# Which sweep takes the fourth destination block: 3, 4, 3, 3 in place of 4, 3, 3, 3 in a chain of dense graph layers

## The reference

```python
x = _layernorm(x + _L0_gnn_ref(...))   # three GCN layers, weighted edges, relu, then a linear layer
x = _layernorm(x + _L1_gnn_ref(...))   # two SAGE layers, mean over neighbours
x = _layernorm(x + _L2_gnn_ref(...))   # encoder, 5 steps of a GRU, decoder
x = _layernorm(x + _L3_gnn_ref(...))   # one GCN layer, edges counted

def step(h, w):                        # the GRU step of L2
    agg = jax.ops.segment_sum((h @ w)[src], dst, num_segments=n_nodes)
    gi, gh = agg @ gru_wih.T + gru_bih, h @ gru_whh.T + gru_bhh
    ...                                # r, z, n from the three thirds of gi and gh
    return ((1.0 - z) * n + z * h, None)
```

## Time and profile before

| | |
|---|---|
| median of three runs | 5918.23 us (5917.7 to 5918.91) |
| profiled execution | 5918.44 us, its span 5916.7 us |
| TensorE matmul busy | 4612.3 us (78%), 24881 matmuls |
| TensorE weight loads busy | 2374.8 us (40%) |
| VectorE / ScalarE / GpSimd busy | 2160.1 / 609.5 / 2625.5 us |
| build of the tables, TensorE mostly idle | until about 1458 us |
| chunk matmuls L780 | 14014 records, 3677.8 us busy |
| DMA | 1401.93 MB, mean 237 GB/s |

### The profile page before, as it was taken

The page is one execution under the profiler, slowest core; times in us unless marked ns, Lnnn a source line. Parts: engine busy times, 40 slices in busy tenths (PEclk is TensorE's granted clock), DMA queues, the critical chain, the costliest instruction groups (busy, mean ns, idle before and its releaser), DMA issues. The chain is left out here.

```text
span 5916.7 us, 76914 instructions
## 1 busy us (share of the span) xinstructions
PE 4612.3 (78%) x24881; PEld 2374.8 (40%) x24881; DVE 2160.1 (37%) x4014; ACT 609.5 (10%) x1331; POOL 2625.5 (44%) x1727
## 2 busy tenths in 40 slices
PE   1222222223999999999999999899999999998796
PEld 1222222222444444444455554444444444443343
DVE  9999999998000000011013111303022120303413
ACT  0000000000011111111111011202011020202300
POOL 3888888888788888888885000000000000000100
PEclk7555555555999999999999999999999999999897
DMA  9999953223999999999989877595867768583474
GB/s 353 357 351 352 350 109 42 36 36 82 314 292 289 297 275 300 289 297 278 300 251 273 279 260 246 162 299 174 272 215 230 249 192 298 167 279 107 132 255 140
DMA packets 717658, 1401.93 MB, mean 237 GB/s; under 512 B 268948, under 2 KB 356840, under 8 KB 692456
## 3 DMA queue, kind: packets, MB, share of 16 engines
q1 hardware_dynamic: 483832, 1346.10, 68.1%
q0 software_dynamic: 225792, 0.70, 7.7%
q10 hardware_dynamic: 7920, 53.79, 2.4%
HBM read 1160.09 MB, written 240.26 MB: 237 GB/s over the span
## 5 line engine op out<-in xcount | busy, mean ns | idle before, releaser
L780 PE MATMUL psum<-arena 128*128 128x512 f16 (+3 forms) x14014 | 3677.8, 424 | 71.1 <-DVE arena L1126 51.0
L780 PEld LDWEIGHTS psum<-arena 128*128 (+2 forms) x14014 | 1670.3, 123 | 2013.4 <-issue 938.5
L495 POOL DMA_INDIRECT W_adj<-arena x784 | 1331.8, 1699 | 295.6 <-issue 253.3
L495 POOL DMA_INDIRECT C_adj<-arena x784 | 1216.2, 1551 | 250.1 <-issue 243.0
L448 PE MATMUL psum<-arena 128*128 (+1 forms) x6664 | 224.1, 167 | 1070.6 <-DVE arena L397 1057.0
L379 DVE TENSOR_SCALAR_CACHE_REDUCE arena<-arena 128x2048 bf16<-128x2048 f32 (+15 forms) x784 | 996.9, 1342 | 0.5 <-issue 0.5
L623 POOL TENSOR_TENSOR arena<-arena 128x512 f32 (+1 forms) x13 | 22.1, 1698 | 1811.7 <-DVE arena L1115 1811.7
L448 PEld LDWEIGHTS psum<-arena 128*128 128x128 bf16 x6664 | 213.6, 104 | 1095.3 <-issue 1013.1
L1299 DVE COPY arena<-psum 128x512 f32<-128x512 f32 (+1 forms) x39 | 23.2, 654 | 1118.6 <-PE psum L790 1023.4
L1301 DVE TENSOR_SCALAR arena<-psum,arena 128x512 f32<-128x512 f32 x30 | 21.9, 748 | 1038.9 <-PE psum L780 1038.9
L621 POOL COPY arena<-arena 128x512 f32 (+1 forms) x13 | 8.0, 616 | 614.0 <-DVE arena L1115 614.0
(11 more groups left out here) (231 smaller groups left out, 2535.1 us busy)
## 6 DMA issues: line engine op xcount, KB each, us to landing
arena<-C_adj SPq DMA_DIRECT2D x784, 384.0 KB
arena<-W_adj SPq DMA_DIRECT2D x294, 768.0 KB
arena<-C_adj SPq DMA_DIRECT2D x392, 512.0 KB
arena<-W_adj SPq DMA_DIRECT2D x147, 1024.0 KB
arena<-C_adj SPq DMA_DIRECT2D x392, 288.0 KB
arena<-W_adj SPq DMA_DIRECT2D x147, 576.0 KB
W_adj<-arena SPq DMA_DIRECT2D x12, 6400.0 KB
W_adj<-arena SPq DMA_DIRECT2D x12, 6144.0 KB
```

The lines of the kernel that those rows point to most:

```text
L495: return pool.indirect_dma_start(table, bass.IndirectOffsetOnAxis(idx[:, t:t + 1], 0), values[:, t:t + 1], None, compute_op=ALU.add)
L780: ins = pe.matmul(psum[:, bank + b, 0:width], lhs, ring[:, slot, b * BANK:b * BANK + width], start=begin and part == 0, stop=False, skip_g ...
```

## The change

The four-block sweep is the second one instead of the first. Sweep 0 covers blocks 0 to 2 in banks 0 to 2, sweep 1 blocks 3 to 6 in banks 4 to 7. The last two sweeps are as before. Sweep 1 now fills bank 7, so the small weight matmuls and their readers move to bank 3, which is free in sweeps 0 and 1. The number of blocks, matmuls and loaded bytes is as before.

```diff
-SWEEPS = ((0, 4, 0), (4, 3, 4), (7, 3, 0), (10, 3, 4))
+SWEEPS = ((0, 3, 0), (3, 4, 4), (7, 3, 0), (10, 3, 4))
+FREE_BANK = 3
...
                     pe.wait_ge(s["features_set"], feat + UNITS)
-                    pe.matmul(psum[:, 7, 0:3 * D], wt[f"cT{NEXT_GRU[name, arg]}"], wih, start=True,
+                    pe.matmul(psum[:, FREE_BANK, 0:3 * D], wt[f"cT{NEXT_GRU[name, arg]}"], wih, start=True,
                               stop=True).then_inc(s["probs_set"], 1)
                 if (name, arg) == ("gcn", 1) and sweep == 0:
...
                     pe.wait_ge(s["abs_set"], 7)
-                    pe.matmul(psum[:, 7, 0:D], ones, abs_w["W1s"], start=True, stop=False)
-                    pe.matmul(psum[:, 7, 0:D], ones, abs_w["W1n"], start=False, stop=True)
+                    pe.matmul(psum[:, FREE_BANK, 0:D], ones, abs_w["W1s"], start=True, stop=False)
+                    pe.matmul(psum[:, FREE_BANK, 0:D], ones, abs_w["W1n"], start=False, stop=True)
...
                     if sweep == 0 and (name, arg) in NEXT_GRU:
                         dve.wait_ge(s["probs_set"], NEXT_GRU[name, arg] + 1)
-                        dve.tensor_copy(gates, psum[:, 7, 0:3 * D])
+                        dve.tensor_copy(gates, psum[:, FREE_BANK, 0:3 * D])
```

More of the change, by code:

```diff
@@ L885, in tensor @@
                     pe.wait_ge(s["abs_set"], 7)
-                    pe.matmul(psum[:, 7, 0:D], ones, abs_w["W1s"], start=True, stop=False)
-                    pe.matmul(psum[:, 7, 0:D], ones, abs_w["W1n"], start=False, stop=True)
-                    pe.matmul(psum[:, 7, D:D + 1], abs_w["E1T"], ones[:, 0:1], start=True, stop=True,
+                    pe.matmul(psum[:, FREE_BANK, 0:D], ones, abs_w["W1s"], start=True, stop=False)
+                    pe.matmul(psum[:, FREE_BANK, 0:D], ones, abs_w["W1n"], start=False, stop=True)
+                    pe.matmul(psum[:, FREE_BANK, D:D + 1], abs_w["E1T"], ones[:, 0:1], start=True, stop=True,
                               skip_group_check=True).then_inc(s["reach_in"], 1)
@@ L891, in tensor @@
                     pe.wait_ge(s["reach_set"], 1)
-                    pe.matmul(psum[:, 7, 2 * D:3 * D], reach1_wide, abs_w["E2T"], start=True, stop=False,
+                    pe.matmul(psum[:, FREE_BANK, 2 * D:3 * D], reach1_wide, abs_w["E2T"], start=True, stop=False,
                               skip_group_check=True)
-                    pe.matmul(psum[:, 7, 2 * D:3 * D], abs_eb2, ident, start=False, stop=True,
+                    pe.matmul(psum[:, FREE_BANK, 2 * D:3 * D], abs_eb2, ident, start=False, stop=True,
                               skip_group_check=True).then_inc(s["reach_in"], 1)
@@ L1268, in vector @@
                         dve.wait_ge(s["reach_in"], 1)
-                        link(dve.scalar_tensor_tensor(out=abs_sb1, in0=psum[:, 7, 0:D], scalar=LN_BOUND, in1=abs_sb1,
+                        link(dve.scalar_tensor_tensor(out=abs_sb1, in0=psum[:, FREE_BANK, 0:D], scalar=LN_BOUND, in1=abs_sb1,
                                                       op0=ALU.mult, op1=ALU.add))
                         dve.tensor_reduce(top_abs[:, 0:1], abs_sb1, AX, ALU.max)
-                        link(dve.scalar_tensor_tensor(out=reach1, in0=psum[:, 7, D:D + 1], scalar=LN_BOUND,
+                        link(dve.scalar_tensor_tensor(out=reach1, in0=psum[:, FREE_BANK, D:D + 1], scalar=LN_BOUND,
                                                       in1=abs_eb1, op0=ALU.mult, op1=ALU.add))
@@ L1276, in vector @@
                         dve.wait_ge(s["reach_in"], 2)
-                        link(dve.tensor_reduce(top_abs[:, 1:2], psum[:, 7, 2 * D:3 * D], AX, ALU.max))
+                        link(dve.tensor_reduce(top_abs[:, 1:2], psum[:, FREE_BANK, 2 * D:3 * D], AX, ALU.max))
                         link(dve.tensor_scalar(top_abs[:, 1:2], top_abs[:, 1:2], 1.0, None, ALU.max))
```

## The result

The changed kernel takes 5950.32 us (median of six runs, 5944.59 to 5952.0); the kernel before, on the same chip, 5918.54 us (six runs, 5917.22 to 5919.58). The ratio is 1.0053, with a 95% interval from 1.004 to 1.0066: 31.8 us slower. The profiled execution took 5948.95 us, its span 5947.2 us. The prediction was 5945.5 us, from 5932 to 5958.

A forecast was written before the change was run, and what follows sets the result against it. Outside first sweeps the matmul count bounds the time; in first sweeps TensorE waits on VectorE and ScalarE chains. Gru 6.9, decode 19.5, gcn 2's first chunk 0.4 and other first chunks 0.5 sum to 27.3 us: 5945.5 us, range 5932 to 5958.

The forecast's parts named there:

- What cancels: All 11 stages: sweep 1 gains 21.1 us (float16) or 42.1 (float32); sweep 0 gives it back where TensorE bounds it.
- Rival 3: Gcn 2 turns to VectorE's pace or an enc answer comes 0.4 us late: 5955 to 5962 us, chance 0.06.
- The term of 0.4 us for gcn 2's first chunk: Start of gcn 2: two matmuls leaving the first chunk lengthen TensorE's wait for ACT L935, 0.4 us.
- the 0.5 for all the others: First chunks of the other seven float16 stages: 0.5 us for all together, bounds 0 and 3.0.
- Gru, 6.9 us: Gru 0 to 3, last unit's transposes: TensorE ready 1.72 us earlier waits for the same L1209, 6.9 us in all.
- Decode, 19.5 us: Decode: sweep 0 gives back only 1.6 of the 21.1 us that sweep 1 gains, cost 19.5.
- The first step: Decode's first three chunks: six matmuls fewer, 1.29 us a unit, only lengthen the wait, from 3.66 to 4.95 us.
- The lower bound: Decode with no excess from the low clock: period 11.87 us, 21.5 us given back, cost about 0.
- Rival 1: Decode's fourth chunk at 2.4 GHz in every unit, so decode costs nothing: 5926 us, inside 0.2%, chance 0.08.
- Rival 2: Half clock lasts through decode's fourth chunk, L719 and L752, or follows gru's new waits: 5969 us, half 5957, chance 0.08.
- Rival 4: Sweep 0 gives nothing back in any stage, running at its chains' pace: 295 us, 6213 us, chance 0.01.
- rival 5: A gain somewhere else, such as a sooner start of a sweep; no size given, chance 0.02.

The follow-up runs named there:

- the second step: Against the changed kernel, float16 stages in sweeps of 2, 4, 4 and 3 blocks instead of 3, 4, 3 and 3: 6034.96 us.
- the kernel with the filled waits: Changed kernel plus 18 unused matmuls into bank 3 ahead of the fourth chunk in each unit of decode's sweep 0: 5927.29 us.
- the version with 5858 us: Kernel before, with decode's sweep 0 reordered so that every unit's four chunks come from the unit before: 5858.32 us.

## Why the prediction was right, and where its numbers were off

**What cancels.** Right. The three float32 stages, gcn 2, sage and enc gave back the moved time; with the new blocks in them alone the ratio is 0.9999, so that a cost of some 5 us either way is all that the interval leaves. The first column of the table of stages allows up to 3 us on the mean (2554.7 in six executions with the new blocks, 2552.1 in four without). Sweep 1 grew by 21.1 to 21.4 us in float16 stages (expected 21.1) without idle time, and sweep 0 of gcn 2, sage and enc shrank by 20.8 to 21.2 (by the distances between the sweeps' last matmuls). Rival 3, that gcn 2 or enc runs out of cover, did not come at this step; the second step shows that both do at one block less. The term of 0.4 us for gcn 2's first chunk is too small to be told from zero; the 0.5 for all the others was too little, as gru shows.

**Gru, 6.9 us.** The wait was forecast at 1.72 us in each of four stages, for the line that was L1209, and came as four waits of 1.6 us there, 6.3 in all. But the part costs 10.7 us timed. The mis-sized term is the one for first chunks, 0.5 us in all, and it fails in two ways. The first is cover again: the prediction took it that most first chunks are followed by data that is long there, and in gru they are not. The changed kernel in gru 2, at full clock:

```profile
4711.06 1.46 PE L781 MATMUL psum<-arena 128*128 128x512 f16 x6 [2.16 <-DVE arena L1229]
4712.79 1.12 PE L727 MATMUL psum<-arena 128*128 x2 [0.28 <-DVE arena L1203]
```

L727 waits for VectorE's L1203 and comes 1.73 us after the chunk's start, as late as it comes in gru 1 behind eight matmuls before. The second is the clock, which was taken as it had been. In gru 1 and 3 the first chunk now starts at half clock behind the same wait as before; in gru 2 it no longer does. Gru 1 before, then after:

```profile
4367.74 1.89 PE L780 MATMUL psum<-arena 128*128 128x512 f16 x8 [2.16 <-DVE arena L1228]
4369.48 0.69 PE L726 MATMUL psum<-arena 128*128 x1
```

```profile
4369.20 2.58 PE L781 MATMUL psum<-arena 128*128 128x512 f16 x6 [2.16 <-DVE arena L1229]
4371.57 1.63 PE L727 MATMUL psum<-arena 128*128 x2
```

Eight matmuls took 1.74 us, six now take 2.37. From the first chunk to the next one it is 9.00, 7.42, 9.00 and 7.42 us in gru 0 to 3 before, and 8.60, 8.57, 7.42 and 8.57 after: 32.8 and 33.2 together. So of the 1.7 us that left these four places nothing came back. Gru 1 costs 3.3 us by the table of stages, gru 3 too, gru 0 1.7 and gru 2 0.6: 8.9 together, 6.3 of it the waits, 2.0 the first chunks, 0.6 not followed. Most of what is missing to the 10.7 is the one more slow unit in gru 4 (1.6 us, 1.4 in the kernel with gru alone), outside of everything that the sum went through. The prediction's bound of 3.0 us for the first chunks holds the 2.0 here; nothing in it held gru 4.

**Decode, 19.5 us.** Timed 19.7 us with the new blocks in decode alone, 20.4 by the traces. The first step, that the six matmuls of the first three chunks only lengthen the wait, holds to 0.2 us (9.72 to 9.82 and 9.91). The second was an excess of 1.7 us at half clock in each unit; the two shown have 3.64 - 2.15 = 1.49 and 4.20 - 2.15 = 2.05, and the mean of ten units is 1.67. That the 1.7 fits so well is in part luck: it was put between two observations made behind other idle times, and the single units range from 1.48 to 2.05. The period lies outside the forecast 13.4 to 13.7 us in two of the ten. Over the whole sweep 1.4 us are given back where 1.6 were predicted. The other 0.7 are in sweep 1, 21.4 us longer instead of 21.1, and in sweep 2, which nobody moved (64.8 to 65.2). The lower bound, an excess of nothing, was given a period of 11.87 us; the kernel with the filled waits has 11.88.

**Rivals.** Rival 1, full clock in decode at 5926 us, is where that kernel stands (5927.3), but the clock was held there by added work; in the changed kernel it was not. Rival 2, a half clock that lasts longer, came in part: it took in L720 (1.70 us for 0.86) and in some units the first of L753, but cost less on the fourth chunk (1.94 and 2.53 us for 1.29, before 3.08 for 1.72), so that the mean excess per unit grew only from 1.43 to 1.67 us. Gru's new wait did not lower the clock: behind 1.58 us of idleness 24 matmuls took 5.18 us (4150.99 to 4156.17), their full pace, and the same in gru 1 to 3. Rival 4, no give-back at all, is excluded by the six stages. There was no gain anywhere for rival 5.

**The sum.** Predicted 27.3 us; measured 31.8 by the medians and 30.5 by the two profiled executions. By the latter the miss of 3.2 is 2.0 in gru, 1.6 in gru 4 and 0.9 in decode, less 1.3 in what was taken for the start, the other first chunks and the ends of the program. The part in gru is the first chunks, lost cover and time at half clock together; the part in gru 4 is time at half clock by the rows shown. The 0.9 of decode is 0.2 in sweep 0, 0.3 in sweep 1 and 0.4 in sweep 2; why the two later sweeps grew, and the last term, were not followed further.

## What to carry to other kernels

Matmuls that are moved out of a phase with round trips are saved there only as far as the phase is bound by TensorE. Before such a move, list for each place what stands between the request and the answer, and take the moved work off that cover: where nothing is left over, the move costs its whole size. The first chunk of a stage is such a place too. Of the independent work that a kernel has, put as much as memory allows into the phase that waits; and where the order within the phase can be changed so that work one unit older covers the chain, as in the version with 5858 us, that can be worth more: here it gained 59.3 us, nearly twice what the split of blocks cost.

## What the chip showed

- More matmuls, less time: 216 matmuls of no use in the waits of one stage made the kernel about 22 us faster, because TensorE stayed at 2.4 GHz (granted clock 0.99 instead of 0.83 over decode's first sweep).
- The same idle time was followed by either level: 2.16 us ahead of gru 1's first chunk by 0.217 us a matmul in one kernel and 0.395 in the other, 1.87 us in gru 4 by full pace in one and a slow stretch in the other. Within one execution too: of gru 4's equal units three or four are slow. So an untouched stage changed by 1.6 us with the work ahead of it. What decides it is left open: no run here was made for it.
- Behind equal waits of 4.77 us the fourth chunk of decode took 1.94 us in one period and 2.53 in the next: the slow stretch doesn't always take in the whole chunk, and its cost per unit is to be read as a mean over units.
